# Second layer norm centred in SBUF, its squares summed by one fp32 product, the second MLP product in another PSUM bank, and PV with 49 weight columns

## The reference, cut to what matters

```python
x = x + conv(_gn(x))                       # depthwise 31 x 31, plus bias
x = x + roll(from_windows(vit(to_windows(roll(_gn(x))))))
def vit(t):                                # t: (windows, 49 tokens, 96)
    h = ln(t) * ln1_s + ln1_b
    q, k, v = h @ wq + bq, h @ wk + bk, h @ wv + bv      # 12 heads of 8
    o = softmax(q @ k.T / sqrt(8)) @ v
    t = t + o @ wo + bo
    h = ln(t) * ln2_s + ln2_b
    return t + gelu(h @ w1 + b1) @ w2 + b2               # 384 wide
```

## Time and profile before

| | us |
|---|---|
| median of 3 runs | 5721.61 |
| lowest and highest run | 5716.38, 5734.21 |
| the profiled execution | 5688.4 |
| its span, first to last instruction | 5686.6 |
| TensorE matmuls busy | 5342.2 (94%) |
| VectorE, ScalarE, GpSimd busy | 3397.2, 3542.0, 3509.3 (60 to 62%) |
| mean granted TensorE clock | 0.976 of 2.4 GHz |

### The profile page before, as it was taken

The page is one execution under the profiler, slowest core; times in us unless marked ns, Lnnn a source line. Parts: engine busy times, 40 slices in busy tenths (PEclk is TensorE's granted clock), DMA queues, the critical chain, the costliest instruction groups (busy, mean ns, idle before and its releaser), DMA issues.

```text
span 5686.6 us, 229687 instructions
## 1 busy us (share of the span) xinstructions
PE 5342.2 (94%) x97360; PEld 4217.5 (74%) x97360; DVE 3397.2 (60%) x5850; ACT 3542.0 (62%) x5590; POOL 3509.3 (62%) x4814
## 2 busy tenths in 40 slices
PE   6999999999599999999999999999999999999998
PEld 6999999999466666666666666666666666666665
DVE  2333333433267677677676777776677777777773
ACT  3444444444367777777776777777777777777775
POOL 2222222222367777777777777777777777777774
PEclk9999999999689999999998999999999999999996
DMA  4444444444356666666665666666666666666662
GB/s 125 116 121 120 127 121 120 116 125 104 71 126 140 140 140 140 140 140 140 140 140 127 139 139 140 140 140 140 140 140 140 140 140 140 140 140 140 140 140 47
DMA packets 1099823, 740.58 MB, mean 130 GB/s; under 512 B 465428, under 2 KB 1070708, under 8 KB 1098708
## 3 DMA queue, kind: packets, MB, share of 16 engines
q1 hardware_dynamic: 1069620, 687.18, 53.6%
q0 software_dynamic: 29184, 38.71, 3.2%
HBM read 409.02 MB, written 316.46 MB: 128 GB/s over the span
## 4 chain that ended last, share of the span: by engine, by line
PE 61%; issue 7%; DVE 3%; ACT 3%; POOL 0%; ACTq 0%; DVEq 0%; POOLq 0%
PE ps_pv L1121 14%; PE ps_ring L1188 8%; PE ps_s L1075 5%; PE ps_ring L1058 4%; PE ps_xc L1163 4%; PE ps_ring L1049 4%; PE ps_t L1075 4%; PE ps_ring L1180 4%; PE ps_ring L1066 4%; PE ps_ring L1060 2%; PE ps_ring L1059 2%; DVE b_rest L983 2%; ACT b_sq_hi L848 2%; PE ps_ring L1149 2%; PE ps_ring L1067 2%
## 5 line engine op out<-in xcount | busy, mean ns | idle before, releaser
L940 DVE TENSOR_REDUCE b_mx<-ps_s 113x12 f32<-113x588 f32 x1024 | 783.9, 766 | 200.6 <-PE ps_s L1075 200.4
L1121 PEld LDWEIGHTS ps_pv<-b_vd,b_probs_t 128*64 128x64 f32 x24576 | 771.1, 140 | 164.0 <-issue 155.1
L840 ACT ACTIVATE b_probs_t<-ps_t 128x588 f32<-128x588 f32 x1024 | 667.7, 652 | 303.0 <-PE ps_t L1075 302.9
L225 POOL TENSOR_SCALAR xn<-xin,aff 96x896 f32<-96x896 f32 x192 | 173.4, 903 | 1072.2 <-DVE aff L375 1059.5
L1121 PE MATMUL ps_pv<-b_vd,b_probs_t 128*64 128x18 f32 x24576 | 822.5, 213 | 0.3 <-issue 0.3
L746 POOL TENSOR_TENSOR b_mid_lo<-b_mid,b_mid_hi 128x392 fp32r<-128x392 f32 x768 | 788.9, 1027 | 43.3
L410 PE MATMUL ps_conv<-blocks_hi,toep_hi 128*128 128x288 f32 (+2 forms) x2880 | 667.2, 313 | 0.0
L410 PE MATMUL ps_conv<-blocks_hi,toep_lo 128*128 128x288 f32 (+2 forms) x2880 | 654.4, 309 | 0.0
L410 PE MATMUL ps_conv<-blocks_lo,toep_hi 128*128 128x288 f32 (+2 forms) x2880 | 653.7, 308 | 0.0
L801 POOL TENSOR_TENSOR b_outs<-b_y,b_xs 96x392 f32<-96x392 f32 x256 | 316.7, 1237 | 445.2 <-DVE b_y L1021 445.2
L282 ACT ACTIVATE toep_hi<-toep 128x640 fp32r<-128x640 f32 x288 | 197.2, 749 | 632.9 <-PE ps_conv L410 616.7
(11 more groups left out here) (142 smaller groups left out, 12423.3 us busy)
## 6 DMA issues: line engine op xcount, KB each, us to landing
stacked_qk<-b_planes SPq DMA_DIRECT2D x512, 220.5 KB, 2.9
b_q_st<-stacked_qk SPq DMA_DIRECT2D x512, 220.5 KB, 4.3
b_k_st<-stacked_qk SPq DMA_DIRECT2D x512, 220.5 KB, 5.6
toep<-filters_padded SPq DMA_DIRECT2D x96, 936.5 KB, 14.0
...
```

Source lines behind the costliest of these rows:

```text
L840: act.activation(pt[:, p, 0:HEADS * TOK].rearrange("k (e n) -> k e n", e=2), ps_t[:, :, 0:HPAIR * TOK], ACT.Exp, scale=float(DH) ** -0.5). ...
L940: dve.tensor_reduce(mx[0:rows_q, :].rearrange("q (e m p) -> q e m p", e=2, p=PAIRS)[:, :, :, p], ps_s[0:rows_q, :, 0:HPAIR * TOK].rearrang ...
L1121: ins = pe.matmul(to, pt[:, p, at:at + WS], vd[:, m % VR, p, h, :, :], start=True, stop=True, skip_group_check=True)
```

## The change

- The second norm: the product with `average` gives the mean of t1 in a ring bank (`mean2`, in place of `w2` in the ring). VectorE subtracts it from t1 into a new SBUF tile `xc2`, ahead of its fourth row maximum. ScalarE squares `xc2` once; `sq2_hi` and `sq2_lo` go. The variance is one fp32 product with `ones_f`, now behind v. `h2_hi` and `h2` read `xc2` instead of `ps_xc`.
- The second MLP product goes into `ps_xc`, and the next step's first-norm product waits for `y_done` of the step before, not for `h2`.
- In the ring q now waits for `t1_done`, k for `xc2`, v for `q_done`, the variance for `k_done`.
- PV loads 49 weight columns instead of 64 and writes 49 rows; `ps_pv` is set to one once so that the unused rows hold numbers.

In the diff the ring comes first, then ScalarE, VectorE and TensorE:

```diff
-                ("q", QKV, "q_done", 1, 1), ("k", QKV, "k_done", 1, 1),
-                ("var2", PROJ, "lg2", 1, 1), ("v", QKV, "v_done", 1, 1),
-                ("w2", MLPS, "y_done", 1, 1)]
+                ("mean2", PROJ, "xc2", 1, 1), ("q", QKV, "q_done", 1, 1),
+                ("k", QKV, "k_done", 1, 1), ("v", QKV, "v_done", 1, 1),
+                ("var2", PROJ, "lg2", 1, 1)]
...
-                    square(i, proj, sq2, "xc2", "sq2", "sq2_split")
-                if proj is not None:
-                    square(i, proj, sq2_hi, "xc2", "sq2_high", "sq2_split", used="var2")
+                    square(i, proj, sq2, xc2[:, :], "xc2", "sq2", ("var2",))
...
+                if proj is not None:
+                    dve.wait_ge(S["mean2"], proj + 1)
+                    after(dve, i, "sq2", proj)
+                    after(dve, i, "h2_high", proj)
+                    after(dve, i, "h2_done", proj)
+                    dve.tensor_tensor(xc2[:, :], t1[:, proj % 2, :], bank(i, s, "mean2")[0:C, 0:NT],
+                                      ALU.subtract).then_inc(S["xc2"], 1)
                 row_max(i, att, 3)
-                if proj is not None:
-                    dve.wait_ge(S["sq2_high"], proj + 1)
-                    dve.wait_ge(S["sq2"], proj + 1)
-                    dve.tensor_tensor(sq2_lo[:, :], sq2[:, :], sq2_hi[:, :].bitcast(F32), ALU.subtract).then_inc(
-                        S["sq2_split"], 1)
...
-                    dve.tensor_tensor(h2_hi[:, :], ps_xc[0:C, 0:NT], rstd[:, :], ALU.mult).then_inc(S["h2_high"], 1)
+                    dve.tensor_tensor(h2_hi[:, :], xc2[:, :], rstd[:, :], ALU.mult).then_inc(S["h2_high"], 1)
...
-                    dve.scalar_tensor_tensor(y[:, mlps % 2, :], bank(i, s, "w2")[0:C, 0:NT], cols[0:C, B2:B2 + 1],
+                    dve.scalar_tensor_tensor(y[:, mlps % 2, :], ps_xc[0:C, 0:NT], cols[0:C, B2:B2 + 1],
...
-                        to = ps_pv[WS * odd:WS * odd + WS, 0:PAIRS * HEADS * VA].rearrange(
+                        to = ps_pv[WS * odd:WS * odd + TOK, 0:PAIRS * HEADS * VA].rearrange(
...
-                        ins = pe.matmul(to, pt[:, p, at:at + WS], vd[:, m % VR, p, h, :, :], start=True, stop=True,
+                        ins = pe.matmul(to, pt[:, p, at:at + TOK], vd[:, m % VR, p, h, :, :], start=True, stop=True,
...
                     pe.wait_ge(S["t0_split"], qkv + 1)
-                    after(pe, i, "h2_done", qkv - (PROJ - QKV))
-                    after(pe, i, "h2_high", qkv - (PROJ - QKV))
+                    after(pe, i, "y_done", qkv - (MLPS - QKV))
...
                     pe.wait_ge(S["t1_done"], proj + 1)
-                    pe.wait_ge(S["h1_done"], qkv + 1 if qkv is not None else BATCH * B)
-                    pe.matmul(ps_xc[0:C, 0:NT], cc("center", C), t1[:, proj % 2, :], start=True,
-                              stop=True).then_inc(S["xc2"], 1)
+                    product(i, s, "mean2", cc("average", C), t1[:, proj % 2, :], C, "mean2")
...
-                if proj is not None:
-                    spread(i, s, proj, "var2", sq2_hi, sq2_lo, "sq2_split", "var2")
...
                     ins.then_inc(S["v_ps"], 1)
+                if proj is not None:
+                    pe.wait_ge(S["sq2"], proj + 1)
+                    product(i, s, "var2", ones_f[:, :], sq2[:, :], C, "var2")
                 if mlps is not None:
-                    wait_bank(pe, i, s, "w2")
+                    pe.wait_ge(S["h1_done"], qkv + 1 if qkv is not None else BATCH * B)
...
-                            ins = pe.matmul(bank(i, s, "w2")[0:C, 0:NT], w[:, m, :], src[:, m, :],
+                            ins = pe.matmul(ps_xc[0:C, 0:NT], w[:, m, :], src[:, m, :],
```

More of the change, by code:

```diff
@@ L501, in window_pass @@
         ones = sb("ones", [C, C], F32R)
+        ones_f = sb("ones_f", [C, C])
         w2 = sb("w2s", [P, NM, C])
@@ L517, in window_pass @@
         sq2 = sb("sq2", [C, NT])
-        sq2_hi = sb("sq2_hi", [C, NT], F32R)
-        sq2_lo = sb("sq2_lo", [C, NT], F32R)
+        xc2 = sb("xc2", [C, NT])
         lg = sb("lg", [C, NT])
@@ L841, in exps, with square @@
                                ps_t[:, :, 0:HPAIR * TOK], ACT.Exp, scale=float(DH) ** -0.5).then_inc(S["exp_done"], 1)
-            def square(i, n, dst, src, done, split, scale=1.0, used=None):
-                act.wait_ge(S[src], n + 1)
-                after(act, i, split, n)
-                if used:
-                    after(act, i, used, n)
-                act.activation(dst[:, :], ps_xc[0:C, 0:NT], ACT.Square, scale=scale).then_inc(S[done], 1)
+            def square(i, n, dst, src, ready, done, used, scale=1.0):
+                act.wait_ge(S[ready], n + 1)
+                for u in used:
+                    after(act, i, u, n)
+                act.activation(dst[:, :], src, ACT.Square, scale=scale).then_inc(S[done], 1)
             def gelu(i, s, n, m, use):
@@ L861, in step @@
                 if qkv is not None:
-                    square(i, qkv, sq1_hi, "xc1", "sq1_high", "sq1_split", 1.0 / C, "var1")
+                    square(i, qkv, sq1_hi, ps_xc[0:C, 0:NT], "xc1", "sq1_high", ("sq1_split", "var1"), 1.0 / C)
                 if qkv is not None:
-                    square(i, qkv, sq1, "xc1", "sq1", "sq1_split", 1.0 / C)
+                    square(i, qkv, sq1, ps_xc[0:C, 0:NT], "xc1", "sq1", ("sq1_split",), 1.0 / C)
                 exps(i, soft, 1)
@@ L1007, in step @@
                     after(dve, i, "h2_split", proj)
-                    dve.tensor_tensor(h2[:, :], ps_xc[0:C, 0:NT], rstd[:, :], ALU.mult).then_inc(S["h2_done"], 1)
+                    dve.tensor_tensor(h2[:, :], xc2[:, :], rstd[:, :], ALU.mult).then_inc(S["h2_done"], 1)
                 if qkv is not None:
```

8 lines of the change are left out of this document (5 added, 3 removed).

## The result

| | before | changed |
|---|---|---|
| median of 4 runs, us | 5718.99 | 7984.59 |
| lowest and highest run, us | 5714.6, 5734.21 | 7961.27, 8009.5 |
| span of the profiled execution, us | 5686.6 | 7974.2 |
| mean granted TensorE clock | 0.976 | 0.658 |

The changed kernel takes 1.396 times as long (95% interval 1.390 to 1.401). The forecast was 7690 us with a range of 6900 to 8050: direction and mechanism came as forecast, the size is 295 us short, near the upper end of the range.

The account below looks back on a forecast made before the run. TensorE, 94% busy with one 0.68 us wait a step, was taken as the bound. Steps growing from 15.8 to 23.8 us over 249 steps add 1992 us, less 13, to 5688.4; median put at 7690 us, range 6900 to 8050.

Parts of the forecast that it names:

- The wait for `y`: Next step's first-norm product waits for VectorE's `y` instead of `h2`; step 17.4 us at full clock, some 2.2 us waiting there.
- the first path: From the first-norm product to the second norm's mean product: 8.53 us at full clock, 9.13 without the PV gain.
- The clock: In the window pass the wait brings TensorE to 1.2 GHz in nearly each step, 0.83 of the time.
- The price of a low microsecond: Each us at 1.2 GHz costs TensorE's work 0.42 us, so work takes 1.7 times as long there.
- The term that failed: With TensorE slower at low clock, 0.8 of the 2.7 us waited in a step stay; step 23.8 us.
- second path: From the second norm's mean product through `y` to the next first-norm product: 8.87 us at full clock.
- `h2_hi` from SBUF: `h2_hi` and `h2` in VectorE reading two SBUF operands: +0 to +0.7 us for the two, taken as 0.
- PV, 0.6 us: PV's weight loads with 49 columns save TensorE 0.3 us a half, 0.6 us a step; bounds 0 to 0.67.
- Rival 1: First-norm product waits for `y` but the clock stays at 2.4 GHz: 17.4 us a step, about 6120 us; chance 0.09.
- rival 2: The clock falls in part of the window-pass steps, every second say: near 20 us a step, 6250 to 6900 us; chance 0.06.
- rival 3: `y` is in time for the first-norm product: 15.0 us a step, about 5520 us; chance 0.03.
- rival 4: PV isn't faster with 49 columns: about +1 us a step at low clock, 24.8 us, 7940 us; no separate chance.

Follow-up runs that it names:

- the run with two products in the wait: Changed kernel plus two fp32 products that no one reads in each step, right ahead of the first-norm product's wait for `y`: 6435.41 us.
- the run with the products elsewhere: Changed kernel plus three fp32 products that no one reads in each step, behind the first MLP product's third part: 8529.4 us.
- the run with the ring: Changed kernel with the second MLP product back in the ring, so the first-norm product waits for neither `y` nor `h2`: 5669.5 us, ratio 0.995.
- the run with the wait alone: Kernel before with one line more: the first-norm product also waits for `y` of the step before: 6876.92 us.

## Why the prediction was right, and where its size was off

- **What bounds the kernel.** TensorE with its one wait of 0.68 us: right for the list of waits, but incomplete. In the run with 49 columns alone the 0.6 us saved on TensorE came back as waits for VectorE, so a second chain was just as long (that it closes through GpSimd is argued); I took TensorE's saved time for saved time, and engines that are not full for engines that cannot hold a step up.
- **The wait for `y`.** Right in place and price: 17.35 us a step at 2.4 GHz (the run with two products in the wait) against 17.4 worked out, and 2.2 us in the steps that reach it at full clock. The sum is a little better than its parts: in the step of 17.41 us the first path takes 4443.74 - 4435.48 = 8.26 us, not 8.53, and the second 9.15, not 8.87, of which 0.2 us is `h2_hi` (0.76 us there).
- **The clock.** Right: low for 0.84 of the window pass against 0.83. That it came so close is partly luck. The share was taken from one pair of stretches where the pipeline runs dry, and the run with the products elsewhere, with the same wait, has a mean clock of 0.63 from 1825 to 8178 us, a share of 0.74. The reason given was right only in part: the falls need no PV behind the wait, and the stretch that I called one of short matmuls has the two first-norm products of 392 columns in it. The Trainium skill's rule on long gaps (TensorE: Matmul & The Clock Gate, Why this matters for your kernels), which warns of long gaps between bursts, would have left the clock alone; waits of 1.3 us bring it down here, and filling them brings it back.
- **The price of a low microsecond**, 0.42, held: with TensorE's 14.7 us and the measured wait of 1.6, the same equation gives (14.7 + 1.6) / (1 - 0.42 x 0.84) = 25.2 us, the measured step.
- **The term that failed** is the 0.8 us of waiting that I left in a step. I had the whole second path at 1.2 GHz, so that a slower TensorE would use up 1.9 of 2.7 us. Where that holds, at 4281.52, 0.81 us stay indeed, though the path (12.12 us) and TensorE's work in it (11.31 us) are each 0.8 us longer than worked out. In most steps the clock is back at 2.4 GHz for the last part of that path (from 4021.95 and 4052.67), just ahead of the wait. TensorE is early again, and 1.59 us stay on the mean. The step is 25.2 us instead of 23.8, and 249 x 1.4 = 350 us is the size of the miss, a little more than the 295 us measured.
- **`h2_hi` from SBUF**: taken at 0, the run with the ring shows 0.94 us at full clock, over the upper bound that I gave for both instructions together. In the changed kernel, where GpSimd is mostly done by then, `h2_hi` takes 0.62 us on the mean, 0.06 more than before; in steps whose products run at full clock by then it is 0.76 to 0.90.
- **PV, 0.6 us**: right as TensorE's work, and worth that only where nothing else is as late.
- **The rivals.** Rival 1 was refuted by the clock, rival 2 appeared in the run with the wait alone; rival 3, `y` in time, did not occur in the changed kernel; rival 4's premise did not hold, but it had about the right size for 64 columns (0.9 us against 1.0).
